# A decoder layer on one Trainium2 core: the softmax exponentials of a sequence joined into one instruction, and the latent attention's values issued one place earlier

## The reference

```python
x = x + local_attention(layernorm(x))           # 16 heads of 16; a latent branch and a gate
x = x + cross_attention(layernorm(x), context)  # 16 heads of 16, causal, relu on q, k, v
x = x + slots(layernorm(x))                     # top-8 routing to 64 slots, GRU
```

## Time and profile before

| | |
|---|---|
| median of 3 runs | 1640.93 us (1639.8 to 1641.42) |
| the profiled execution | 1646.24 us, its span 1644.5 us |
| PE busy | 1538.9 us, 94% of the span, 19038 matmuls |
| PEld busy | 1107.0 us, 67% |
| DVE busy | 1155.0 us, 70% |
| ACT busy | 959.7 us, 58% |
| POOL busy | 859.9 us, 52% |

### The profile page before, as it was taken

One profiled execution on the slowest core, in us unless ns is written; L12 is line 12 of the kernel. 1 busy time (PEld: TensorE's weight loads), 2 busy tenths in 40 slices (PEclk: granted clock), 3 DMA queues, 4 the chain that ended last, 5 costly groups with the idle time before them and its releaser, 6 DMA issues. The chain is left out here.

```text
span 1644.5 us, 52068 instructions
## 1 busy us (share of the span) xinstructions
PE 1538.9 (94%) x19038; PEld 1107.0 (67%) x19038; DVE 1155.0 (70%) x2897; ACT 959.7 (58%) x1926; POOL 859.9 (52%) x1178
## 2 busy tenths in 40 slices
PE   5999999999999999996999999999999958999997
PEld 4677776777777677764677777777777635666664
DVE  5667777677777677762576767667676737998986
ACT  2555555555555555543666675766667516777773
POOL 2454444554444544433376666667666643555553
PEclk7999999999999999996999999999999968999998
DMA  5300000000000000002100000000000000000001
GB/s 158 117 2 1 0 0 0 0 0 0 0 0 0 0 0 0 1 2 84 42 15 20 13 13 19 13 19 13 19 13 13 3 0 7 33 32 32 32 32 39
DMA packets 31202, 32.31 MB, mean 20 GB/s; under 512 B 3937, under 2 KB 29602, under 8 KB 31138
## 3 DMA queue, kind: packets, MB, share of 16 engines
q1 hardware_dynamic: 31138, 31.46, 6.2%
HBM read 23.06 MB, written 8.39 MB: 19 GB/s over the span
## 5 line engine op out<-in xcount | busy, mean ns | idle before, releaser
L1455 DVE TENSOR_REDUCE c_neg_max<-score_banks 128x16 f32<-128x2048 f32 x64 | 146.6, 2290 | 98.5 <-PE score_banks L1229 98.5
L998 POOL TENSOR_TENSOR a_less<-a_attn,a_remote 128x512 f32<-128x512 f32 x32 | 40.7, 1273 | 265.2 <-DVE a_attn L846 265.2
L984 POOL TENSOR_SCALAR_AFFINE_SELECT a_probs_t<-a_probs_t 128x512 f32<-128x512 f32 x256 | 158.0, 647 | 33.5 <-ACT a_probs_t L669 33.4
L669 ACT ACTIVATE a_probs_t<-score_banks 128x512 f32<-128x512 f32 x256 | 135.7, 601 | 48.6 <-PE score_banks L513 48.6
L826 DVE TENSOR_REDUCE a_neg_max<-score_banks 128x16 f32<-128x2048 f32 x64 | 146.4, 2288 | 21.0 <-PE score_banks L481 21.0
L1564 POOL TENSOR_SCALAR_AFFINE_SELECT c_probs_t<-c_probs_t 128x512 f32<-128x512 f32 x256 | 154.8, 639 | 9.7 <-ACT c_probs_t L1383 9.7
L1383 ACT ACTIVATE c_probs_t<-score_banks 128x512 f32<-128x512 f32 x256 | 132.3, 602 | 17.5 <-PE score_banks L1257 15.8
L361 PE MATMUL side_banks<-a_xn_t,a_w_qk 128*128 128x256 f32 x512 | 133.9, 396 | 1.3 <-ACT a_xn_t L613 1.3
L361 PEld LDWEIGHTS side_banks<-a_xn_t,a_w_qk 128*128 128x128 f32 x512 | 92.9, 196 | 11.1 <-ACT a_xn_t L613 1.7
L1575 POOL TENSOR_TENSOR c_scaled<-c_normed,gamma 128x512 f32<-128x512 f32 x32 | 40.6, 1268 | 97.7 <-DVE c_normed L1438 97.7
L1836 PE MATMUL side_banks<-w_ih,gi_t 128*128 128x512 f32 (+1 forms) x256 | 88.3, 487 | 0.4 <-DVE n_in L2002 0.2
(11 more groups left out here) (254 smaller groups left out, 4192.1 us busy)
## 6 DMA issues: line engine op xcount, KB each, us to landing
x_sb<-in_x SPq DMA_DIRECT2D x32, 256.0 KB, 2.9
c_ctx_in<-in_ctx SPq DMA_DIRECT2D x32, 256.0 KB, 2.7
out<-y SPq DMA_DIRECT2D x32, 256.0 KB, 2.1
w_ih<-in_ffn_w_ih SPq DMA_DIRECT2D x1, 768.0 KB, 6.8
w_hh<-in_ffn_w_hh SPq DMA_DIRECT2D x1, 768.0 KB, 7.7
a_raw_qk<-in_attn_qk_w SPq DMA_DIRECT2D x1, 512.0 KB, 3.5
a_raw_cross<-in_xattn_qk_w SPq DMA_DIRECT2D x1, 512.0 KB, 4.4
b_ih<-in_ffn_b_ih SPq DMA_DIRECT2D x1, 384.0 KB, 6.2
```

Source lines behind the costliest of these rows:

```text
L669: nc.scalar.activation(probs_t[tt][:, 4 * g:4 * g + 4, :].rearrange("p j q -> p (j q)"), score_banks[:, g, :], ACT.Exp, scale=SCALE).then_ ...
L984: nc.gpsimd.affine_select(out=probs, in_=probs, pattern=[[0, 4], [1, 128]], compare_op=ALU.is_ge, fill=0.0, base=-1, channel_multiplier=-1 ...
L1455: nc.vector.tensor_reduce(neg_max[:, tt, :], all_scores, AX.X, ALU.max, negate=True).then_inc(max_done, 1)
```

## The change

In both attentions the four exponentials of a sequence become one over all four banks, 2048 columns, with one increment of `exp_done`; its count goes from eight a pair to two. `scores(prev, 0)` waits once instead of four times before it overwrites the banks, with one increment of `pe_turn` instead of four. `scores_t(prev, 1)` waits once for the whole exponential of the first sequence. GpSimd waits once in front of its four masks.

In the first attention `lat_values(prev)` stands ahead of `project_v(at, 1)` in PE's queue, where it stood behind it, and both copies of `copy_lat_out` stand ahead of the second sequence's exponential in ScalarE's.

```diff
@@ first layer, TensorE: scores (the second layer's is changed alike)
+                if tt == 0:
+                    wait(pe, exp_done, at.count(2, 0))
+                    pe.sem_inc(pe_turn, 1)
                 for i in range(4):
-                    if tt == 0:
-                        wait(pe, exp_done, at.count(8, i - 3))
-                        pe.sem_inc(pe_turn, 1)
                     for c in range(4):
@@ both layers, TensorE: scores_t
                 if tt == 0:
                     pe.wait_ge(max_done, at.count(2, 2))
+                else:
+                    pe.wait_ge(exp_done, at.count(2, 1))
                 toks = slice(S * tt, S * tt + S)
                 for j in range(4):
                     for i in range(4):
-                        if tt == 1 and j == 0:
-                            pe.wait_ge(exp_done, at.count(8, i + 1))
@@ first layer, TensorE: step
                     scores_t(prev, 1)
+                if prev.real:
+                    lat_values(prev)
                 if at.real:
                     project_v(at, 1)
-                if prev.real:
-                    lat_values(prev)
@@ both layers, ScalarE: exp (the second layer's had its four in a loop)
-            def exp(at, tt, g):
-                if g == 0:
-                    act.wait_ge(sct_filled, at.count(2, tt + 1))
-                    wait(act, av_filled, at.count(2, tt - 1))
-                nc.scalar.activation(probs_t[tt][:, 4 * g:4 * g + 4, :].rearrange("p j q -> p (j q)"),
-                                     score_banks[:, g, :], ACT.Exp, scale=SCALE).then_inc(exp_done, 1)
+            def exp(at, tt):
+                act.wait_ge(sct_filled, at.count(2, tt + 1))
+                wait(act, av_filled, at.count(2, tt - 1))
+                nc.scalar.activation(probs_t[tt][:].rearrange("p h q -> p (h q)"),
+                                     score_banks[:].rearrange("p b n -> p (b n)"), ACT.Exp,
+                                     scale=SCALE).then_inc(exp_done, 1)
@@ first layer, ScalarE: step
                 if prev.real:
-                    for g in range(4):
-                        exp(prev, 0, g)
+                    exp(prev, 0)
...
                 if prev.real:
-                    exp(prev, 1, 0)
-                    exp(prev, 1, 1)
                     copy_lat_out(prev)
-                    exp(prev, 1, 2)
-                    exp(prev, 1, 3)
+                    exp(prev, 1)
@@ both layers, GpSimd: mask_weights
+                pool.wait_ge(exp_done, at.count(2, tt + 1))
+                pool.sem_inc(pool_turn, 1)
                 for g in range(4):
-                    pool.wait_ge(exp_done, at.count(8, 4 * tt + g + 1))
-                    pool.sem_inc(pool_turn, 1)
```

## The result

| | before | after |
|---|---|---|
| median | 1640.37 us (1639.76 to 1641.42, 4 runs) | 1626.97 us (1626.49 to 1628.31, 4 runs) |
| ratio | | 0.9919, 95% interval 0.9907 to 0.9932 |
| profiled execution, span | 1644.5 us | 1624.8 us |

What follows compares the result with a forecast made beforehand. TensorE, busy nearly the whole span, was taken as the bound, with VectorE setting the first layer's first stretch. Terms 7.5 + 3.1 + 1.9 - 0.7 = 11.8 us off the 1640.93 median gave 1629.1 us, range 1624.5 to 1637.5.

Steps and rivals of the forecast that it cites:

- Second layer, 3.1 + 1.9 = 5.0 us: Second layer: unstretched mask loads save 0.24 us x 13 turns; the single exponential's earlier end saves 0.06 us x 31 pairs.
- the hold by POOL's masks: Second layer: the short pair's 0.43 us hold of values(old, 1) appears in the long pair too, leaving 0.22 us gained.
- 0.02 for masks that end earlier: Second layer: 0.02 us added to the long pair's 0.22 us gain for masks ending a bit earlier, 0.24 us in all.
- First layer, 7.5 us: First layer: moved latent values and earlier ScalarE copies bring project_out forward 0.25 us a pair, in about 30 pairs.
- `values(prev, 0)` waits for this (`v_ready`) and starts at about 318.09: First layer: VectorE's bias on V, ending at 318.05, holds values, which starts 0.04 us later and eats the shape-change saving.
- The first rival: First layer gives nothing because V's bias comes 0.25 us later than thought; 4.3 us left, 1636.6 us, chance 0.15.
- I let `copy_mix` wait for TensorE's transposes (319.82): First layer, ScalarE: the mix copy starts when transposes L547 are filled, is done at 320.44; project_out at 320.48, not 320.73.
- The exponential, 1.83 us: Both layers, ScalarE: one exponential over 2048 columns takes 1.83 us, bounds 1.3 and 2.06, where four take 2.06.
- The drain rule: Changing tiling mode drains TensorE; one change less is worth 0.36 us. As full-collection rival: 15.5 us, 1625.4 us, chance 0.08.
- The end of the second layer, 0.7 us lost: End of second layer: the exponential's first-quarter signal comes 1.2 us later, delaying POOL's masks; at most 1.2 us, 0.7 taken.
- Slow exponential: Rival, both layers: the single exponential is slow; at 2.25 us the kernel is 3.3 us slower, 1644 us, chance 0.05.
- stretch that stays: Rival, second layer: mask loads stay stretched because the branch causes it, not the waits; 8.7 us left, 1632.2 us, chance 0.12.

Runs made afterwards that it cites:

- e4: Kernel before with the second layer's part alone, but four exponentials a sequence and one exp_done increment behind the fourth: 1638.20 us, ratio 0.9976.
- e2: Kernel before with one exponential a sequence and its waits in the first layer only, latent values unmoved, latent copies behind the second exponential: 1642.83 us, ratio 0.9996.
- e9: Changed kernel with both latent copies behind the second sequence's exponential on ScalarE, latent values still ahead of project_v: 1639.23 us, ratio 0.9985 to the kernel before.
- e1: Kernel before with only the first layer's latent values and latent copies moved ahead, four exponentials and their waits kept: 1637.16 us, ratio 0.9962.
- e5: Changed kernel with copy_mix(old) ahead of evac_av(prev, 0) in ScalarE's row of the first layer: 1624.99 us, ratio 0.9889 to the kernel before.
- e7: Changed kernel with VectorE's lat_norm behind the second row maximum and second normalise in the first layer: 1621.73 us, ratio 0.9864 to the kernel before.
- e8: Changed kernel with the three moves of e5, e6 and e7 together: 1608.23 us, ratio 0.9787 to the kernel before.
- e6: Changed kernel with GpSimd's second-sequence masks in the second layer right behind the first's, ahead of both deviations: 1620.37 us, ratio 0.9861 to the kernel before.

## Why the prediction was right, and where it was wrong

- **Second layer, 3.1 + 1.9 = 5.0 us: right in sum and mechanism.** The trace gives 4.8, but the terms are 2.2 and 2.6 (e4), so here two small errors cancelled. The loop takes 13 turns, yet the kernel before has only 12 long pairs: they stand behind the 12 jumps back, and behind the thirteenth branch, which leaves the loop (1272.2), the mask loads take 0.14 us; and the single exponential is worth 0.08 us a pair and not 0.06. The pairs went to one length, 16.73, the stretch left with the wait steps (e4), and the hold by POOL's masks appeared in the long pair as forecast. The "0.02 for masks that end earlier" isn't seen apart.
- **First layer, 7.5 us: too small.** The trace gives 0.33 us a pair, 9.7 us over the 29 pairs in the windows above. The step that failed is "`values(prev, 0)` waits for this (`v_ready`) and starts at about 318.09". The bias computed in a step belongs to pair `at`, the values to `prev`, whose V was ready a step earlier; the wait in the code carries `prev`'s count. L528 was to come 0.04 us later and came 0.19 us earlier (2.36 us behind L513 instead of 2.55). The copy that L528 does wait for is ScalarE's first latent copy. In a full pair of the kernel before it cost next to nothing (a gap of 0.20 us, 0.17 after the change), in the last pair 0.81 us. I was led by that last pair, where the profile names VectorE as the releaser. The rows of VectorE and ScalarE there, in the kernel before:

```profile
723.10 0.44 DVE L792 TENSOR_TENSOR a_v_heads<-side_banks,a_b_v 128x272 f32<-128x272 f32 x1 [1.99 <-PE side_banks L406]
723.55 0.63 ACT L651 ACTIVATE a_lat_out<-side_banks,ident 128x128 f32<-128x128 f32 x2 [0.47 <-PE side_banks L439]
```

  VectorE was done at 723.54; L528 loaded at 723.99, 0.45 us later. It stands 0.44 us behind the start of the first copy (723.55), and in the full pair of the earlier trace rows again 0.44 us (318.05 - 317.61). e2 and e9 settle it: with the copies behind the exponential L528 moves with them. The first rival (nothing from the first layer) rested on the same misread row.
- **The missed row on ScalarE.** I let `copy_mix` wait for TensorE's transposes (319.82). Since those came earlier than forecast, ScalarE's row became the bound: L555 starts when the copies behind the exponential are through. So the exponential's length matters in the first layer too (e1, 0.18 us a pair), and swapping two copies gives 0.13 us more (e5).
- **The exponential, 1.83 us: 1.88 measured**, 64 times in each layer, against 2.06 for four. The Trainium skill's "ScalarE: Activation LUTs", section What ACT_TABLE_LOAD costs, gave an estimate of 1.89, and the trace agrees with it.
- **The drain rule** of the Trainium skill's "TensorEngine Tiling (Array Packing)", section Key Properties: the gaps agree, 0.32 us into 64\*32 as assumed. One change of shape less takes away the 0.36 us gap, but L355, now directly behind L406 in the same shape, takes 0.59 us where it took 0.42. L528 came 0.19 us earlier in all, 0.03 of it from the copy, so the full 0.36 us are not there even for TensorE alone.
- **The end of the second layer, 0.7 us lost:** not tested. The masks of the last exponential end 1302.75 + 2.39 - 1300.71 = 4.43 us after its start, and ended 1320.67 + 2.40 - 1319.51 = 3.56 us after it before: 0.87 us later, inside the bound of 1.2. Whether that reaches the end can't be read: the stretch from the last pair to the end is 1.1 us shorter after, with another share at the lower clock.
- Slow exponential, stretch that stays, nothing from the first layer: none of the rivals happened. The sum of 11.8 us is below the 13.4 of the medians mainly by the first layer's term. That this term came near is in part luck: the wait that was to limit it never happened, and what did the limiting, ScalarE's row up to the mix copy, was bounded by TensorE in the forecast.

## What to carry to other kernels

A releaser that the profile names is an inference: check its end time, and read in the code which iteration's count the wait carries. Ask of each engine what its row looks like after the change, since the saved wait of one engine ends where the next engine's row begins; here neither a shape change saved on TensorE nor a shorter exponential was worth anything while ScalarE's latent copies stood behind the exponential, be the latent values moved (e9) or not (e2). When pairs of a loop alternate in length, look in the longer one: here it led to the wait steps on TensorE (e4) and to VectorE's order (e7). And ask again what holds each stretch once a change is in: the three moves of e8 gave more (18.7 us between the two medians) than the change itself.

## What the runs showed that I had not expected

- One exponential of 128x2048 across four PSUM banks takes 1.88 us, four of 128x512 take 2.06 us: only 0.06 us for each of three starts saved. One alone takes 0.60 us, so four in a row already overlapped by about 0.12 us each.
- Four waits with increments between sixteen small weight loads on TensorE cost 0.40 us, but only in the pair right behind the loop's jump back; elsewhere 0.14 us with or without them.
- With POOL's masks out of the way (e6) the second layer's pairs alternate again, 16.38 and 16.57 us, on a VectorE wait: L1249 behind `c_neg_max`, 0.35 and 0.54 us.
- The gap at a change of shape out of 128\*128 goes with the columns of the matmuls ahead of it, not with the shape changed to. In the pairs of the kernel before, the gap from 128\*128 into 32\*32 is 0.17 us behind 128 fp32 columns (L1167), 0.33 behind 256 (L555, L1173) and 0.36 behind 272 (L449), and into 64\*32 it is 0.36 behind 272 too (L406).
